# Earlier weight conversions on ScalarE and other PSUM banks for the context, in a graph-network, linear-attention and feed-forward kernel

## The chip, the cores and the metric

The kernel runs on one core of one Trainium2 chip, as a single launch. The metric is the device time of one execution in microseconds (us), lower is better; the time of a version is the median of its runs.

The core has five engines that run side by side and meet only at semaphores: TensorE (PE in the profile; its weight loads are the row PEld), VectorE (DVE), ScalarE (ACT), GpSimd (POOL) and SyncE (SP), which here issues the transfers from memory. TensorE writes to PSUM, which has eight banks.

## The reference, cut to what matters

There are 1250 rows of 512 features. The rows are normalized, and then go through two branches whose results are added to the input; a feed-forward block follows. The change touches the second branch, a linear attention with 8 heads of 64:

```
def mix(x, w_qkv, w_out, b_out, ln_scale):            # x is (1, 1250, 512)
    q, k, v = jnp.split(einsum('bnc,cf->bnf', x, w_qkv), 3, axis=-1)   # then 8 heads of 64
    q = softmax(q, axis=-1) / sqrt(64)                 # over the 64 features of a head
    k = softmax(k, axis=1);  v = v / N                 # over the 1250 rows
    context = einsum('bnhd,bnhe->bhde', k, v)          # 64 x 64 per head
    out = einsum('bhde,bnhd->bhen', context, q)        # back to (1, 1250, 512)
    out = einsum('bnf,fc->bnc', out, w_out) + b_out
    return (out - mean) * rsqrt(var + eps) * ln_scale
```

The first branch is a graph network. It needs `segment_sum(x[src], dst)` twice, over 41250 edges, and the kernel does that as a product with a 1250 x 1250 matrix of edge counts, which it builds itself while the other products run.

## The kernel before, in words

Every product is done with operands that are split in two float16 parts, a high one and a low one, so each block of a product is three matmuls (`passes`, L447 to L457). The 1250 rows are 10 tiles of 125, or 5 chunks of 250.

**Weights.** Ten matrices of 512 x 512 pass one after the other through one staging buffer, in the order `lin, up0, k, q, v, out, down0, up1, down1, gate`. For each, SyncE issues the load into `stage` (L395) once the matrix before has been split, ScalarE scales it in place (L746) and writes the high half to one of three slots (L756), and GpSimd writes the low half (L1639), which frees `stage` for the next load. ScalarE and GpSimd do this at fixed places of their own instruction streams, written out by hand. `wait_slot` keeps ScalarE from writing a slot whose former matrix may still be read.

**The edge counts.** The matrix is built in 25 windows of 50 columns. For a window, VectorE makes the start columns and the one-hot operands (L1105 to L1117, five instructions), TensorE reads the 16 start columns into registers and does one matmul that clears the bank (L440) and 16 small ones (L443), and ScalarE copies the sum out (L767). Windows alternate between banks 6 and 7. Four windows lie among the tiles of `up0`, six in the key stage, ten in the value stage, five in the last stage of the attention.

**The stages around the change**, in order:

- *Key stage*: TensorE does 20 blocks of keys with a window after every third, VectorE moves each block out of PSUM and keeps its maximum. Then VectorE takes the maxima together (`kneg`, L1280), and ScalarE takes four exponentials (L864) that TensorE waits for before it transposes the keys.
- *Query and value stage*: the order of tiles is the list `QV`: queries 0 to 6, then value 0, query 7, value 1, query 8, value 2, query 9, values 3 to 9. They use banks 0 to 3 in turn (family `z`). VectorE subtracts the maximum per head from a query tile (L1291, L1292), ScalarE takes its exponential, VectorE sums it (L1296, L1297), and GpSimd multiplies by the reciprocal (L1657, for all ten tiles, behind the split of `out` in its stream). With each of queries 2 to 6 TensorE transposes two key tiles into banks 4 and 5 (family `x`, L518), ScalarE writes their high half (L780) and VectorE the low one (L1127). A value tile goes out by ScalarE (L877) and VectorE (L1127). The window of a value tile lies behind the next value tile on TensorE (L564), and ahead of the tile's low half on VectorE (L1308).
- *Context*: two halves of 60 matmuls each, then two query tiles transposed by `flip_q` (L508), then four projections (`m`, L587 to L590) of the context with `out`, which use banks 0 and 1 in turn. The halves lie in banks 4 and 5, which the transposed query tiles use next.
- *Last stage of the attention*: ten tiles with the projected matrix, five windows; then the graph layers.

Of the kernel before, what the change touches and what calls it, by code (L numbers as in the profile page):

```python
# [30 lines left out]
T = N // P  # L31
# [42 lines left out]
SLOTS = 3  # L74
# [9 lines left out]
Q_FIRST, KN_LAG = 7, 2  # L84
QV = [("q", _t) for _t in range(Q_FIRST)]
for _t in range(T):
# [6 lines left out]
    "z": [("qv", 2 * T, "dve", 0)],  # L93
# [3 lines left out]
    "x": [("xn", T, "dve", 1), ("up0", T, "dve", 1), ("kn", T, "dve", 1), ("ctx", 2, "dve", 1), ("qt", T, "dve", 1),  # L97
# [44 lines left out]
READER = {"lin": ("t", "lin"), "up0": ("x", "up0"), "k": ("t", "k"), "q": ("z", "qv"), "v": ("z", "qv"), "out": ("n", "m"),  # L142
# [3 lines left out]
def gps_block(nc, dram):  # L146

    with ExitStack() as ctx:
# [203 lines left out]
        def wait_slot(eng, i):  # L352

            if i >= SLOTS:
                family, phase = READER[WEIGHTS[i - SLOTS]]
                eng.wait_ge(full[family], before(family, phase) + entry(family, phase)[1])
# [65 lines left out]
        def _(pe):  # L422
# [147 lines left out]
            for b in range(2):  # L570
                wait_bank(pe, "x", "ctx", b, b)
                for q in range(2):
                    part = slice((2 * b + q) * 128, (2 * b + q + 1) * 128)
                    last = passes(bank("x", b)[:, q * 128:(q + 1) * 128], lambda h, t: v_nat[:, h, t, part],
                                  lambda h, t: k_nat[:, h, t, part], T)
                last.then_inc(full["x"], 1)
# [163 lines left out]
        def _(act):  # L740
# [118 lines left out]
            for i in range(WINDOWS["k"]):  # L859
                window("k", i)  # L860

# [4 lines left out]
            split_weight("v")  # L866

            for i, (kind, t) in enumerate(QV):
                if kind == "q":
# [4 lines left out]
                    nc.scalar.activation(q_nat[:, t, :], q_nat[:, t, :], ACT.Exp, scale=S_XW).then_inc(q_exp, 1)  # L874
                else:
# [3 lines left out]
                    if t == 0:  # L879
                        split_weight("out")  # L880
# [3 lines left out]
            for b in range(2):  # L884
                wait_full(act, "x", "ctx", b)
                for hh in range(2):
                    part = slice(hh * DH, hh * DH + DH)
                    last = nc.scalar.activation(ctx16[part, 0, 2 * b:2 * b + 2, part],
                                                bank("x", b)[part, 0:256].rearrange("p (q d) -> p q d", q=2)[:, :, part],
                                                ACT.Copy, scale=1 / (S_X * S_K))  # L890
                last.then_inc(high["x"], 1)
# [190 lines left out]
        def _(dve):  # L1082
# [233 lines left out]
            for b in range(2):  # L1316
                wait_high(dve, "x", "ctx", b)
                for hh in range(2):
                    part = slice(hh * DH, hh * DH + DH)
                    last = low(ctx16[part, 1, 2 * b:2 * b + 2, part],  # L1320
                               bank("x", b)[part, 0:256].rearrange("p (q d) -> p q d", q=2)[:, :, part],
                               ctx16[part, 0, 2 * b:2 * b + 2, part], 1 / (S_X * S_K))
                last.then_inc(free["x", "dve"], 1)
# [455 lines left out]
```

## Time and profile before

| | before |
|---|---|
| median of 3 runs | 530.96 us (530.7 to 535.82) |
| the profiled execution | 531.56 us, of which the profile's span is 529.8 us |
| TensorE busy | 478.6 us, 90% of the span |
| weight loads of TensorE busy | 363.3 us, 69% |
| VectorE, ScalarE, GpSimd busy | 323.4 us (61%), 251.7 us (48%), 166.1 us (31%) |
| chain that ended last | TensorE 73%, VectorE 13%, ScalarE 9%, issue 3% |
| mean granted clock of TensorE | 0.96 of full speed |

In the profile the place of an instruction is its line in the program, so one of a helper stands for all who call it: L454 is every float16 product, L1127 every low half that is made from a scaled source. A name such as `r` or `late` is a memory region whose parts hold different matrices at different times; `ps` is PSUM.

### The profile page before, as it was taken

What the parts mean: (1) busy time and instruction counts of PE and PEld (TensorE: products, weight loads), DVE (VectorE), ACT (ScalarE), POOL (GpSimd) and SP (SyncE); (2) the same over time, 40 slices, a digit from 0 to 9 for tenths busy, and PEclk for the clock granted to TensorE, in tenths of its full rate; (3) what the DMA queues carried; (4) which work ended last, traced back from release to release, by engine and by line L of the source; (5) the groups of instructions that cost most, each with busy time, mean ns of one, the idle gap of its engine ahead of it and who ended that gap; (6) DMA issues with size and microseconds to landing.
All of it is one profiled execution on the core that took longest, in us unless ns stands there. A gap on an engine that the chain in (4) does not pass through costs nothing.

```text
span 529.8 us, 10016 instructions
## 1 busy us (share of the span) xinstructions
PE 478.6 (90%) x3589; PEld 363.3 (69%) x3589; DVE 323.4 (61%) x737; ACT 251.7 (48%) x526; POOL 166.1 (31%) x176
## 2 busy tenths in 40 slices
PE   2989999997997997997999995999999978989893
PEld 1767558875764665664899993668999857866641
DVE  4667698746969855863453536644333376439777
ACT  4778334137451345153235553534336377743344
POOL 1469154003039103033124990002321323303502
PEclk9989999999999989998899997999999957999998
DMA  8602001200102002002100001000000295000015
GB/s 245 188 2 79 1 12 70 81 1 29 51 2 80 2 1 79 2 6 84 74 0 0 2 1 58 1 0 1 0 0 1 83 396 240 1 0 1 1 41 153
DMA packets 5245, 27.42 MB, mean 52 GB/s; under 512 B 1036, under 2 KB 1161, under 8 KB 3544
## 3 DMA queue, kind: packets, MB, share of 16 engines
q1 hardware_dynamic: 5208, 26.92, 14.7%
q8 instruction: 24, 0.39, 0.3%
q14 instruction: 13, 0.11, 0.1%
HBM read 24.36 MB, written 2.56 MB: 51 GB/s over the span
## 4 chain that ended last, share of the span: by engine, by line
PE 73%; DVE 13%; ACT 9%; issue 3%; POOL 1%; DMA 1%; SPq 0%; ACTq 0%; DVEq 0%
PE ps L454 45%; PE ps L612 17%; PE ps L443 5%; PE ps L704 2%; PE ps L508 2%; DVE r L1126 1%; PE ps L440 1%; ACT wslot L756 1%; DVE r L1578 1%; PE ps L518 1%; DVE stat L1148 1%; DVE r L1590 1%; POOL late L1631 1%; DVE r L1568 1%; ACT late L864 1%
## 5 line engine op out<-in xcount | busy, mean ns | idle before, releaser
L454 PE MATMUL ps<-r,wslot 128*128 128x250 f16 x840 | 97.7, 277 | 4.4 <-DVE r L1126 4.3
L454 PEld LDWEIGHTS ps<-r,wslot 128*128 128x128 f16 x840 | 83.1, 100 | 16.9 <-DVE r L1126 5.9
L612 PE MATMUL ps<-late,r 125*128 (+1 forms) x800 | 89.7, 274 | 3.8 <-issue 3.8
L612 PEld LDWEIGHTS ps<-late,r 125*128 125x128 f16 x800 | 78.8, 99 | 15.0 <-issue 4.5
L1639 POOL TENSOR_TENSOR wslot<-stage,wslot 128x512 f16<-128x512 f32 x32 | 39.4, 1261 | 155.7 <-ACT wslot L756 155.7
L454 PE MATMUL ps<-wslot,r 128*125 128x512 f16 x300 | 69.4, 382 | 0.0
L454 PE MATMUL ps<-wslot,late 128*125 128x512 f16 x240 | 56.3, 389 | 6.3 <-DVE late L1418 5.9
L1667 POOL TENSOR_TENSOR late<-ohs,late 128x250 f16<-128x250 f32 x40 | 25.6, 651 | 99.2 <-ACT late L929 99.2
L454 PEld LDWEIGHTS ps<-wslot,r 128*125 128x125 f16 (+1 forms) x300 | 39.4, 137 | 22.2 <-issue 2.3
L454 PE MATMUL ps<-late,wslot 128*128 x480 | 51.5, 270 | 0.0
L454 PEld LDWEIGHTS ps<-wslot,late 128*125 128x125 f16 x240 | 32.8, 140 | 25.2 <-issue 7.5
L767 ACT ACTIVATE late<-ps 125x500 f16<-125x500 f32 x25 | 14.7, 587 | 74.0 <-PE ps L443 74.0
L454 PEld LDWEIGHTS ps<-late,wslot 128*128 128x128 f16 x480 | 46.7, 97 | 4.5
L1399 DVE TENSOR_SCALAR ohs<-ohs,cols 128x250 f32<-128x250 f32 x40 | 16.1, 405 | 48.3 <-ACT ohs L924 48.3
L924 ACT ACTIVATE ohs<-ps,bias_a 128x250 f32<-128x250 f32 x40 | 18.5, 466 | 37.1 <-PE ps L612 29.9
L1127 DVE SCALAR_TENSOR_TENSOR r<-ps,r 125x512 f16<-125x512 f32 (+1 forms) x30 | 20.4, 684 | 22.7 <-ACT r L780 14.9
L780 ACT ACTIVATE r<-ps 125x512 f16<-125x512 f32 x20 | 12.0, 599 | 39.1 <-PE ps L454 39.1
L1107 DVE TENSOR_TENSOR ohs<-iota,sources 125x2048 f16<-125x2048 f16 x25 | 30.4, 1218 | 0.1
L1438 DVE BATCH_NORM_STATS2 stat<-r x32 | 13.3, 421 | 26.4 <-ACT r L973 26.4
L443 PE MATMUL ps<-ohs 125*128 125x80 f16 x400 | 28.4, 205 | 0.9 <-DVE ohs L1117 0.8
L443 PEld LDWEIGHTS ps<-ohs 125*128 125x128 f16 x400 | 21.9, 99 | 10.0 <-issue 6.7
L973 ACT ACTIVATE r<-ps,cols 128x250 f32<-128x250 f32 x40 | 18.3, 465 | 19.4 <-PE ps L454 19.4
(181 smaller groups left out, 745.3 us busy)
## 6 DMA issues: line engine op xcount, KB each, us to landing
late<-in_tv SPq DMA_DIRECT2D x2, 4096.0 KB, 17.5
x<-in_x SPq DMA_DIRECT2D x5, 448.0 KB
out<-r SPq DMA_DIRECT2D x10, 224.0 KB
stage<-in_w_up SPq DMA_DIRECT2D x2, 1024.0 KB, 5.8
stage<-in_w_down SPq DMA_DIRECT2D x2, 1024.0 KB, 4.7
stage<-in_w_lin SPq DMA_DIRECT2D x1, 1024.0 KB, 6.5
stage<-in_w_k SPq DMA_DIRECT2D x1, 1024.0 KB, 4.8
stage<-in_w_q SPq DMA_DIRECT2D x1, 1024.0 KB, 4.9
```

The lines of the kernel that those rows point to most:

```text
L443: mm_ = nc.tensor.matmul(ps[:, 6 + slot, bass.ds(at[c], SPAN)], oh_s[:, slot, c, :], oh_d[:, slot, c, :], start=False, stop=(c == WC - 1))
L454: last = nc.tensor.matmul(out, stat_(hs, b), mov(hm, b), start=start and n == 0, stop=stop and n == 3 * blocks - 1)
L612: last = nc.tensor.matmul(bank("t", m), u_nat[layer][:, p, h, m * 128:(m + 1) * 128], counts(h)[:, chunk], start=(start and h == 0 and p = ...
L767: nc.scalar.activation(adj[:, :, w * WIN:(w + 1) * WIN], ps[0:P, 6 + w % 2, 0:WK].rearrange("p (d h) -> p h d", h=T), ACT.Copy, accum_out= ...
L924: nc.scalar.activation(act_tmp[:, m, :], bank("t", m), ACT.Identity, bias=bias_a[:, KB * layer + m:KB * layer + m + 1], scale=S_H / S_X).t ...
L973: nc.scalar.activation(gnn_t[:, m, j * CH:(j + 1) * CH], bank("t", m), ACT.Identity, bias=col("b2", KB * layer + m), scale=1 / (S_W * S_H) ...
L1107: nc.vector.tensor_tensor(oh_s[:, slot].rearrange("p c (s r) -> p c s r", r=RUN), iota_s.unsqueeze(1).to_broadcast([P, WC, 128 // RUN, RUN ...
L1127: return nc.vector.scalar_tensor_tensor(out, src, scale, hi, ALU.mult, ALU.subtract)
L1399: nc.vector.tensor_scalar(negative[:, q, :], act_tmp[:, q, :], 0.0, col("conv_a", layer), ALU.min, ALU.mult).then_inc(neg_ready, 1)
L1438: ins = nc.vector.bn_stats(bn_stat[:, m, bass.ts(j, 6)], gnn_t[:, m, bass.ts(j, CH)])
L1639: last = nc.gpsimd.tensor_tensor(wslot[:, i % SLOTS, 1, k, :], stage[:, k * D:(k + 1) * D], wslot[:, i % SLOTS, 0, k, :], ALU.subtract)
L1667: nc.gpsimd.tensor_tensor(a_t[:, 1, m, chunk], act_tmp[:, m, :], a_t[:, 0, m, chunk], ALU.subtract).then_inc(tmp_free, 1)
```

## The change

It has three parts.

1. ScalarE splits `v` two windows before the end of the key stage's windows (after window 4 of 0 to 5) and no longer after the exponentials of the keys. It scales `out` after the exponential of query 5 and writes its high half after that of query 6, and no longer after window 0 of the value stage. GpSimd's stream and SyncE's are as before; they follow as their waits are met.
2. The two halves of the context lie in banks 2 and 3 (`z`), and no longer in 4 and 5 (`x`). The four projections each wait for the half that they read, and no longer all for both.
3. `wait_slot` lets `down0` be written to its slot once the last query is computed, and no longer once the last value is; the place of that split in ScalarE's stream is as before.

```
 USES = {
-    "z": [("qv", 2 * T, "dve", 0)],
+    "z": [("qv", 2 * T, "dve", 0), ("ctx", 2, "dve", 1)],
...
-READER = {... "q": ("z", "qv"), ...}
+READER = {... "q": ("z", "qv", QV.index(("q", T - 1)) + 1), ...}
...
             for b in range(2):
-                wait_bank(pe, "x", "ctx", b, b)
+                wait_bank(pe, "z", "ctx", b, 2 + b)
                 for q in range(2):
                     part = slice((2 * b + q) * 128, (2 * b + q + 1) * 128)
-                    last = passes(bank("x", b)[:, q * 128:(q + 1) * 128], ...)
-                last.then_inc(full["x"], 1)
+                    last = passes(bank("z", 2 + b)[:, q * 128:(q + 1) * 128], ...)
+                last.then_inc(full["z"], 1)
...
             wait_weight(pe, "out")
-            wait_done(pe, "x", "ctx", 2)
             for p in range(KB):
+                wait_done(pe, "z", "ctx", p // 2 + 1)
                 wait_bank(pe, "n", "m", p, p % 2)
...
             for i in range(WINDOWS["k"]):
                 window("k", i)
+                if i == WINDOWS["k"] - 2:
+                    split_weight("v")
...
-            split_weight("v")
 
             for i, (kind, t) in enumerate(QV):
                 if kind == "q":
...
                     nc.scalar.activation(q_nat[:, t, :], q_nat[:, t, :], ACT.Exp, scale=S_XW).then_inc(q_exp, 1)
+                    if t == Q_FIRST - 2:
+                        scale_weight("out")
+                    if t == Q_FIRST - 1:
+                        high_weight("out")
                 else:
...
                     window("v", t)
-                    if t == 0:
-                        split_weight("out")
```

The reads of the context by ScalarE and VectorE, and the semaphores that they raise, are changed from `x` to `z` in the same way.

ScalarE's stream at the end of the key stage, before (L767 copies windows out, L864 is the exponentials of the keys, L746 and L756 scale a matrix and write its high half, L874 is the exponential of a query):

```order
L767 ACTIVATE late,adj_sum<-ps 125x10x50 x6
L864 ACTIVATE late,ksum<-late,kneg 128x1250 x4
L746 ACTIVATE stage<-stage 128x2048
L756 ACTIVATE wslot<-stage 128x2048
L874 ACTIVATE r<-r 125x512 x2
```

The same place of the changed kernel (its line 866 is the former L864, its 875 the former L874):

```order
L767 ACTIVATE late,adj_sum<-ps 125x10x50 x5
L746 ACTIVATE stage<-stage 128x2048
L756 ACTIVATE wslot<-stage 128x2048
L767 ACTIVATE late,adj_sum<-ps 125x10x50
L866 ACTIVATE late,ksum<-late,kneg 128x1250 x4
L875 ACTIVATE r<-r 125x512 x2
```

The pair of L746 and L756 has moved from behind the four exponentials to ahead of the sixth window's copy. Further on in ScalarE's stream, from the key tiles of query 6 on, before (L780 is a key tile, L877 a value tile):

```order
L780 ACTIVATE late<-ps 125x512 x2
L874 ACTIVATE r<-r 125x512
L877 ACTIVATE late<-ps 125x512
L767 ACTIVATE late,adj_sum<-ps 125x10x50
L746 ACTIVATE stage<-stage 128x2048
L756 ACTIVATE wslot<-stage 128x2048
L874 ACTIVATE r<-r 125x512
L877 ACTIVATE late<-ps 125x512
```

The same place of the changed kernel, from the exponential of query 5 on (its line 882 is the former L877):

```order
L875 ACTIVATE r<-r 125x512
L746 ACTIVATE stage<-stage 128x2048
L780 ACTIVATE late<-ps 125x512 x2
L875 ACTIVATE r<-r 125x512
L756 ACTIVATE wslot<-stage 128x2048
L882 ACTIVATE late<-ps 125x512
L767 ACTIVATE late,adj_sum<-ps 125x10x50
L875 ACTIVATE r<-r 125x512
L882 ACTIVATE late<-ps 125x512
```

The scaling of `out` now stands ahead of the last two key tiles, its high half ahead of value 0, and nothing stands between the first value window and query 7. TensorE's instructions are the same in number and order; at the context its waits differ (`free` semaphores of the two families of banks):

```order
-L454 MATMUL ps<-late 128x128 [waits x_free_dve]
+L454 MATMUL ps<-late 128x128 [waits z_free_dve]
 L454 MATMUL ps<-late 128x128 x59
 L508 MATMUL ps<-ident,r 128x125 [waits x_free_dve,q_soft]
...
-L454 MATMUL ps<-wslot,ctx 128x512 [waits n_free_dve,z_free_dve,x_free_dve,w_split]
+L454 MATMUL ps<-wslot,ctx 128x512 [waits n_free_dve,z_free_dve,w_split]
 L454 MATMUL ps<-wslot,ctx 128x512 x2
```

The rows of the transposes (L508) read as before, but the context's own reads no longer count among what their `x` semaphore waits for.

## Rows read from the trace of the kernel before

**Rows 1.** The page, part 4: the chain that ended last, by engine.
```profile
PE 73%; DVE 13%; ACT 9%; issue 3%; POOL 1%; DMA 1%; SPq 0%; ACTq 0%; DVEq 0%
```

**Rows 2.** Timeline of TensorE: start, duration, instruction, count, idle before and its releaser.
```profile
123.17 1.04 PE L518 MATMUL ps<-ident,late 128*125 128x128 f32 x8
124.04 2.75 PE L454 MATMUL ps<-wslot,r 128*125 128x512 f16 x12
129.69 1.21 PE L518 MATMUL ps<-ident,late 128*125 128x128 f32 x8 [2.89 <-DVE late L1127]
```

**Rows 3.** Timeline of ScalarE, key stage to query 5.
```profile
114.24 0.59 ACT L767 ACTIVATE late<-ps 125x500 f16<-125x500 f32 x1 [4.65 <-PE ps L443]
...
121.57 1.89 ACT L746 ACTIVATE stage<-stage 128x2048 f32<-128x2048 f32 x1
...
125.31 1.13 ACT L874 ACTIVATE r<-r 125x512 f32<-125x512 f32 x2
...
137.42 1.08 ACT L780 ACTIVATE late<-ps 125x512 f16<-125x512 f32 x2 [1.82 <-PE ps L518]
```

**Rows 4.** Timeline of VectorE, query 2 and the first key tiles.
```profile
126.79 0.64 DVE L1291 TENSOR_REDUCE qmax<-ps 125x8 f32<-125x512 f32 x1
...
128.07 0.68 DVE L1296 TENSOR_REDUCE qsum<-r 125x8 f32<-125x512 f32 x1
...
128.90 1.24 DVE L1127 SCALAR_TENSOR_TENSOR late<-ps,late 125x512 f16<-125x512 f32 x2
```

**Rows 5.** Timeline of SyncE's queue.
```profile
91.89 0.33 SPq L395 DMA_DIRECT2D stage<-in_w_v  x1
```

**Rows 6.** DMA issues: KB each, median us from issue to landing.
```profile
stage<-in_w_v SPq DMA_DIRECT2D x1, 1024.0 KB, 4.7
```

**Rows 7.** Timeline of GpSimd: the split of out, the ten query tiles.
```profile
154.58 4.50 POOL L1639 TENSOR_TENSOR wslot<-stage,wslot 128x512 f16<-128x512 f32 x4 [24.61 <-ACT wslot L756]
159.04 14.70 POOL L1657 TENSOR_TENSOR r<-r,qsum  x10
```

**Rows 8.** Timeline of VectorE, value windows 0, 1 and 2.
```profile
143.77 0.17 DVE L1105 TENSOR_SCALAR base<-heads 125x16 f32 x1
...
146.14 0.69 DVE L1127 SCALAR_TENSOR_TENSOR late<-ps,late 125x512 f16<-125x512 f32 x1
...
155.54 0.69 DVE L1127 SCALAR_TENSOR_TENSOR late<-ps,late 125x512 f16<-125x512 f32 x1 [4.15 <-ACT late L877]
...
158.30 0.81 DVE L1105 TENSOR_SCALAR base<-heads 125x16 f32 x1
...
162.90 0.68 DVE L1127 SCALAR_TENSOR_TENSOR late<-ps,late 125x512 f16<-125x512 f32 x1
```

**Rows 9.** Timeline of ScalarE, after value window 0.
```profile
150.66 1.90 ACT L746 ACTIVATE stage<-stage 128x2048 f32<-128x2048 f32 x1
```

**Rows 10.** Timeline of TensorE, value stage.
```profile
149.88 5.37 PE L454 MATMUL ps<-wslot,r 128*125 128x512 f16 x24
...
162.38 0.37 PE L440 MATMUL ps<-iota,zeros 1*128 1x500 f16 x1 [0.93 <-issue]
163.12 2.12 PE L443 MATMUL ps<-ohs 125*128 125x80 f16 x16 [0.38 <-DVE ohs L1117]
...
175.26 2.01 PE L443 MATMUL ps<-ohs 125*128 125x80 f16 x16
177.19 2.77 PE L454 MATMUL ps<-wslot,r 128*125 128x512 f16 x12
...
180.21 0.75 PE L443 MATMUL ps<-ohs 125*128 125x80 f16 x16
```

**Rows 11.** Timeline of TensorE, second query transpose behind the context.
```profile
204.03 0.62 PE L508 MATMUL ps<-ident,r 125*128 125x125 f32 x4 [0.93 <-DVE ctx L1127]
```

**Rows 12.** Busy time of each engine by stretch, then granted clock (PEclk), DMA share, GB/s.
```profile
182.00:195.00 13.00, 12.20 (x103) 7.69 (x102) 9.86 (x20) 3.74 (x11) 0.00 (x0) 0.94 0.01 1
195.00:203.00 8.00, 8.00 (x124) 7.87 (x121) 0.58 (x2) 5.12 (x8) 3.60 (x4) 0.88 0.01 2
```

More of the change, by code:

```diff
@@ L139 @@
 assert WINDOWS["up0"] == T - UP_LAG and WINDOWS["k"] == (KB * J - 1) // K_EVERY and WINDOWS["v"] == T and WINDOWS["mix"] < T - 3
-READER = {"lin": ("t", "lin"), "up0": ("x", "up0"), "k": ("t", "k"), "q": ("z", "qv"), "v": ("z", "qv"), "out": ("n", "m"),
+READER = {"lin": ("t", "lin"), "up0": ("x", "up0"), "k": ("t", "k"), "q": ("z", "qv", QV.index(("q", T - 1)) + 1), "v": ("z", "qv"), "out": ("n", "m"),
           "down0": ("t", "down0"), "up1": ("x", "up1"), "down1": ("t", "down1"), "gate": ("t", "gate")}
@@ L354, in wait_slot @@
             if i >= SLOTS:
-                family, phase = READER[WEIGHTS[i - SLOTS]]
-                eng.wait_ge(full[family], before(family, phase) + entry(family, phase)[1])
+                family, phase, *uses = READER[WEIGHTS[i - SLOTS]]
+                eng.wait_ge(full[family], before(family, phase) + (uses[0] if uses else entry(family, phase)[1]))
         def weight(name):
@@ L570, in _ @@
             for b in range(2):
-                wait_bank(pe, "x", "ctx", b, b)
+                wait_bank(pe, "z", "ctx", b, 2 + b)
                 for q in range(2):
                     part = slice((2 * b + q) * 128, (2 * b + q + 1) * 128)
-                    last = passes(bank("x", b)[:, q * 128:(q + 1) * 128], lambda h, t: v_nat[:, h, t, part],
+                    last = passes(bank("z", 2 + b)[:, q * 128:(q + 1) * 128], lambda h, t: v_nat[:, h, t, part],
                                   lambda h, t: k_nat[:, h, t, part], T)
-                last.then_inc(full["x"], 1)
+                last.then_inc(full["z"], 1)
             def flip_q(t):
@@ L888, in _ @@
                     last = nc.scalar.activation(ctx16[part, 0, 2 * b:2 * b + 2, part],
-                                                bank("x", b)[part, 0:256].rearrange("p (q d) -> p q d", q=2)[:, :, part],
+                                                bank("z", 2 + b)[part, 0:256].rearrange("p (q d) -> p q d", q=2)[:, :, part],
                                                 ACT.Copy, scale=1 / (S_X * S_K))
-                last.then_inc(high["x"], 1)
+                last.then_inc(high["z"], 1)
             high_tile_t("qt", q_t, 0, S_Q)
@@ L1320, in _ @@
                     last = low(ctx16[part, 1, 2 * b:2 * b + 2, part],
-                               bank("x", b)[part, 0:256].rearrange("p (q d) -> p q d", q=2)[:, :, part],
+                               bank("z", 2 + b)[part, 0:256].rearrange("p (q d) -> p q d", q=2)[:, :, part],
                                ctx16[part, 0, 2 * b:2 * b + 2, part], 1 / (S_X * S_K))
-                last.then_inc(free["x", "dve"], 1)
+                last.then_inc(free["z", "dve"], 1)
             low_tile_t("qt", q_t, 0, S_Q)
```

6 lines of the change are left out of this document (3 added, 3 removed).

## The prediction

> **What bounds the kernel now.** I read the chain of work that ended last first: it is TensorE for 73% of the span, and VectorE, ScalarE and issue for most of the rest [rows 1]. So an edit that moves work on ScalarE pays only where TensorE stands idle because of it. I then read TensorE's timeline from the key stage to the context for its idle times, and at each the timelines of the engine that ended it. Three places answer to the change. At 129.69 TensorE has stood idle for 2.89 us, until VectorE had made the low half of the first key tile [rows 2]. In the value stage windows 2, 3 and 4 are late: at window 2 TensorE waits 0.93 and 0.38 us, and its 16 small matmuls take 2.12 us, where those of window 5, ready long before, take 0.75 us [rows 10]. And at 204.03 it waits 0.93 us for VectorE to be done with the second half of the context [rows 11].
>
> **Part 1, the split of v.** ScalarE needs 1.89 us to scale and, with the high half, ends 3.74 us after it began: 121.57 to 125.31 [rows 3]. These 3.74 us stand between the exponentials of the keys and those of the queries. In their new place the cover is the idle time of 4.65 us ahead of the last key window's copy at 114.24 [rows 3], from 109.6 to 113.4; so they cost nothing there, and would cost at most 3.74 us if TensorE's windows came closer. The data are there: the load was issued at 91.89 and lands 4.7 us later, at about 96.6 [rows 5, 6].
>
> Without them the first two query exponentials begin at 121.6. VectorE can then start query 2 as soon as TensorE has it, at 123.2 plus about 0.2. It needs 1.28 us for the shift (126.79 to 128.07), 0.83 us for a sum (128.07 to 128.90) and 0.62 us for each low half [rows 4]. First key tile free at 123.4 + 1.28 + 0.83 + 0.62 = 126.1. TensorE does query 3 from 124.04 and is ready for the next transposes at about 126.6 [rows 2]. So the 2.89 us wait goes wholly, and with it the 0.2 us by which the transposes of a stalled pass last longer (1.21 against 1.04 us): **3.1 us**. Next late is nothing: VectorE is then 0.5 us ahead. GpSimd's split of v comes with it, from 125.5 to about 113.5, where VectorE's maximum of the keys (at 116) could be held by it for one of its instructions, 1.12 us (4.50 us for four) [rows 7]. That eats the 0.5 us and some 0.3 us more. Ends: 2.8 and 3.2.
>
> **Part 1, the split of out.** Its two halves go to queries 5 and 6. There ScalarE idles 1.82 us before each pair of key tiles [rows 3], and scaling takes 1.90 us [rows 9], the high half as long: each fits within 0.1 us, with the first value tile perhaps 0.4 us later, which VectorE does not feel since it makes value window 0 first. Where it stood, after window 0 (150.66, 1.90 us twice), it held back the high half of value 1, and VectorE waited 4.15 us for that at 155.54 [rows 8, 9]. That wait goes. But TensorE loses only what makes it late, so I laid the two engines out step by step, all 3.1 us (rounded to 3.2) earlier to begin with:
>
> VectorE starts value window 0 at 140.6. A window takes it 2.37 us alone (143.77 to 146.14), and 4.60 us while GpSimd works through (158.30 to 162.90) [rows 8]. GpSimd splits out from 141.3 to 145.8 and then has six query tiles waiting, at 1.47 us each [rows 7]: it is busy until about 157.6. So I take 4.2, 4.4, 3.7, 2.9 and 2.9 us for windows 0 to 4, between these two ends by GpSimd's share of each. Between two windows lie 2.76 us (155.54 to 158.30) [rows 8], after the last query 1.4. The one-hot operands are then ready at 144.8, 151.9, 158.4, 164.1 and 168.4.
>
> TensorE has value 1 done at 145.8. A pair of tiles is 5.3 us, a window 0.9, or 2.3 when its operands come only just ahead (2.12 or 2.01 against 0.75) [rows 10]. Window 0 at 145.8, window 1 at 152.1, window 2 at 158.6 and late (2.3), value 4 until 163.6, window 3 held to 164.5 and late, value 5 until 169.3, window 4 partly late (1.3). Value 6 starts at 170.6, and before it was at 177.19 [rows 10]. That is 6.6 us earlier, 3.1 of which are known: **3.5 us** for the split of out. Ends: all five windows at 4.60 us give value 6 at 175.5 (1.4 us lost again); never late gives 166.4 (7.6 us won). I take the middle one, since the rows say for how long GpSimd is busy.
>
> From here each value tile costs TensorE more than it costs VectorE, and all later splits and loads hang on TensorE's progress: what follows moves as a block.
>
> **Parts 2 and 3.** With the context in banks of its own, the second query transpose needs nothing from VectorE: 0.93 us go [rows 11]. The projections that follow could begin yet earlier, but their copies queue behind the same reads on ScalarE and VectorE, so the shorter wait for half the context adds nothing: **0.9 us**, ends 0 and 1.9. Banks 2 and 3 were last used by values 8 and 9, which the context waits for anyway. The earlier slot for down0 costs and brings nothing: its split stands behind the last window in ScalarE's stream, when all values have been computed.
>
> **The sum.** 3.1 + 3.5 + 0.9 = 7.5 us. The profiled execution took 531.56 us, so it would be 524.1; the median shown is 0.6 lower, which gives 523.5 us.
>
> **A rule against it.** The trace shows GpSimd's work making VectorE's window 2.23 us longer, which is about 1.5 of its instructions of 1.47 us [rows 7, 8]; the loss sits on the short scalar operations and on the last comparison.
>
> The Trainium skill (SBUF — State Buffer, "SBUF: two separate sides") says that the pair of ports which VectorE and GpSimd share is an exclusive lock, held for a whole instruction, also against a VectorE instruction with two inputs in SBUF. By that rule all five instructions of a window could be held, not only some.
>
> **Rivals.**
> - *VectorE becomes the bound of the value stage.* For: the split of out and the query tiles now meet windows 0 to 4, not 1 to 4. Against: GpSimd has a fixed amount to do. If each window takes 4.60 us the stage gives 1.4 us back: 3.1 - 1.4 + 0.9 = 2.6, or 528.4 us. Chance 0.10.
> - *Each of the five instructions is held.* At half a GpSimd instruction (0.73 us) each, a window is 2.37 + 3.7 = 6.0 us while GpSimd is busy (windows 0 and 1) and 3.1 us after; value 6 then starts at about 173.8, 3.4 us earlier. With the context's 0.9 that is 4.3, or 526.7 us. Against it: 4.60 us is what the row has. Chance 0.07. This is the case of the rule named above.
> - *The windows are in time.* If GpSimd's share is smaller than I have it, up to 10.8 + 0.9 = 11.7 us: 519.3 us. Chance 0.07.
> - *Slower, by the clock.* Between 182 and 203 TensorE was granted its lower level, 1.2 instead of 2.4 GHz, for a part of the time, after a stretch in which it was busy 12.20 of 13 us; over the two stretches that cost 0.06 x 13 + 0.12 x 8 = 1.7 us [rows 12]. Three windows stay late in my count, and idle time at them could bring more such falls. From five more the gain is gone, with six it is 2.7 us slower, 533.7 us. Against: the changed stretch has less idle time than the one before. One fall more or less stays in my range. Chance 0.03.
> - *The split of v misses its gap,* and nothing is saved in front: 7.5 - 3.1 = 4.4, or 526.6 us. Against: both the data and the idle time are in the rows. Chance 0.03.
>
> My forecast has 0.70. Its own range is 521 to 526 (the ends of the key part, 1.7 us of clock, 1.5 us in the value stage). With the rivals, 520.4 to 528.2 holds 8 in 10. About 1% is 5.3 us, what a measurement of this kernel can tell from no change: faster 0.78 (the forecast and the in-time case, little of the others), within it 0.18, slower 0.04.
>
> **What would show it.** In the changed profile: no idle time before the transposes of key tiles 2 and 3, and those at about 126.6; ScalarE's conversion of v between its fifth and sixth key window; no wait of VectorE for value 1's high half; VectorE's windows 0 to 2 near 4 us each; windows 2 and 3 still slow on TensorE; value 6 near 170.6; no wait of the transposes for the context. The forecast is wrong if value 6 starts after 173 or before 168, or if TensorE's granted clock differs over more than some 7 us of the span.

## The result and the profile after

The changed kernel took 525.21 us (median of 4 runs, 524.54 to 526.75); the kernel before took 533.29 us beside it (4 runs, 530.7 to 535.82). The ratio is 0.9857 [0.9812, 0.9903]: faster by 1.4%. Measured again in two later series, the unchanged text of the changed kernel gave 524.55 us at 0.9879 [0.9843, 0.9915] and 524.34 us at 0.9847 [0.9809, 0.9884]. The forecast was 523.5 us, in a range of 520.4 to 528.2.

The profiled execution took 525.78 us with a span of 523.2 us, 6.6 us less than the span of before (529.8). The page's head and its chain by engine:

```profile
PE 477.9 (91%) x3589; PEld 363.3 (69%) x3589; DVE 325.3 (62%) x737; ACT 251.5 (48%) x526; POOL 167.6 (32%) x176
...
PE 79%; DVE 10%; ACT 6%; issue 2%; POOL 1%; DMA 1%; SPq 0%; ACTq 0%; DVEq 0%
```

The chain stands on TensorE for 79% of the span, where it was 73% [rows 1]; what has shrunk is VectorE's part (13% to 10%) and ScalarE's (9% to 6%). TensorE's instructions are the same; the place of ScalarE's conversions and the waits were edited.

**Key and query stage.** ScalarE's timeline around the last key window:

```profile
109.46 1.90 ACT L746 ACTIVATE stage<-stage 128x2048 f32<-128x2048 f32 x1
111.40 1.91 ACT L756 ACTIVATE wslot<-stage 128x2048 f16<-128x2048 f32 x1
114.27 0.59 ACT L767 ACTIVATE late<-ps 125x500 f16<-125x500 f32 x1 [0.96 <-PE ps L443]
...
121.60 1.29 ACT L875 ACTIVATE r<-r 125x512 f32<-125x512 f32 x2
```

The conversion of v sits in what was 4.65 us of idle time [rows 3] and leaves 0.96 us of it; the window's copy starts at 114.27 instead of 114.24, and the first exponentials of the queries at 121.60 instead of 125.31. On TensorE the wait of 2.89 us [rows 2] is gone:

```profile
123.20 1.04 PE L518 MATMUL ps<-ident,late 128*125 128x128 f32 x8
...
126.66 1.04 PE L518 MATMUL ps<-ident,late 128*125 128x128 f32 x8
127.54 2.75 PE L454 MATMUL ps<-wslot,r 128*125 128x512 f16 x12
```

**Value stage.** TensorE, in the same view as rows 10. L440 opens a window, L443 are its 16 small matmuls, whose addresses are read from registers; windows 0 to 4 start in these rows:

```profile
145.79 0.38 PE L440 MATMUL ps<-iota,zeros 1*128 1x500 f16 x1
146.10 0.98 PE L443 MATMUL ps<-ohs 125*128 125x80 f16 x16
...
152.62 1.56 PE L443 MATMUL ps<-ohs 125*128 125x80 f16 x16
...
159.71 1.19 PE L443 MATMUL ps<-ohs 125*128 125x80 f16 x16
...
164.79 0.37 PE L440 MATMUL ps<-iota,zeros 1*128 1x500 f16 x1 [1.16 <-issue]
165.09 2.10 PE L443 MATMUL ps<-ohs 125*128 125x80 f16 x16
167.08 4.19 PE L454 MATMUL ps<-wslot,r 128*125 128x512 f16 x12
...
171.51 0.75 PE L443 MATMUL ps<-ohs 125*128 125x80 f16 x16
172.09 1.27 PE L454 MATMUL ps<-wslot,r 128*125 128x512 f16 x5
```

Value 6 starts at 172.09, 5.1 us earlier than before [rows 10] and 1.5 us later than forecast. Only window 3 still waits. Value 5, at 167.08, lasts 4.19 us where a value tile takes 2.78: TensorE was at its lower level (1.2 GHz) for most of it (mean granted clock 0.57 from 166 to 170). The slow matmuls of windows 0 to 2 are not the clock's: it was 1.00 from 144 to 166.

VectorE, window 0, the first row of window 1 and the low half behind it, and two rows of window 4; L1108, L1110, L1115, L1117 and L1120 are the five instructions of a window:

```profile
140.57 0.17 DVE L1108 TENSOR_SCALAR base<-heads 125x16 f32 x1
140.65 1.22 DVE L1110 TENSOR_TENSOR ohs<-iota,sources 125x2048 f16<-125x2048 f16 x1
141.78 1.12 DVE L1115 TENSOR_SCALAR offsets<-base 1x16 int32<-1x16 f32 x1
...
143.16 1.67 DVE L1120 TENSOR_TENSOR ohs<-iota,rel 125x1280 f16<-125x1280 f16 x1
...
147.50 0.49 DVE L1108 TENSOR_SCALAR base<-heads 125x16 f32 x1
...
151.78 0.68 DVE L1130 SCALAR_TENSOR_TENSOR late<-ps,late 125x512 f16<-125x512 f32 x1
...
167.28 1.01 DVE L1115 TENSOR_SCALAR offsets<-base 1x16 int32<-1x16 f32 x1
...
168.55 0.82 DVE L1120 TENSOR_TENSOR ohs<-iota,rel 125x1280 f16<-125x1280 f16 x1
```

From the start of the base to the start of the low half, windows 0 to 4 last 4.18, 4.28, 4.06, 3.27 and 3.77 us (in the last, 0.42 us is idle time behind the five instructions). The wait of 4.15 us for value 1's high half [rows 8] is gone. GpSimd:

```profile
113.38 4.50 POOL L1642 TENSOR_TENSOR wslot<-stage,wslot 128x512 f16<-128x512 f32 x4 [21.58 <-ACT wslot L756]
141.21 5.75 POOL L1642 TENSOR_TENSOR wslot<-stage,wslot 128x512 f16<-128x512 f32 x4 [23.33 <-ACT wslot L756]
146.92 11.06 POOL L1660 TENSOR_TENSOR r<-r,qsum  x8
161.63 1.94 POOL L1660 TENSOR_TENSOR r<-r,qsum  x1 [3.65 <-DVE qsum L1300]
166.32 1.94 POOL L1660 TENSOR_TENSOR r<-r,qsum  x1 [2.75 <-DVE qsum L1300]
```

Its share of the split of out takes 5.75 us and not 4.50. With eight query tiles it is busy until 157.98, near the forecast (157.6). But the last two query tiles are each released by VectorE's reciprocal (L1300), which stands immediately ahead of a window. So windows 3 and 4 meet one GpSimd instruction each. That I had not seen.

**Context.** TensorE behind it:

```profile
197.97 1.03 PE L508 MATMUL ps<-ident,r 125*128 125x125 f32 x8
198.83 1.46 PE L454 MATMUL ps<-wslot,ctx 128*128 128x512 f16 x6
201.40 1.47 PE L454 MATMUL ps<-wslot,ctx 128*128 128x512 f16 x6 [1.11 <-issue]
```

Both transposes run as one group of 8, with no wait between them, where 0.93 us stood [rows 11].

**The account.** I cut the span at the starts of fixed pieces of TensorE's work. Behind each stretch, in brackets, is an estimate of what the lower level cost TensorE in it, the stretch times one minus its granted clock. It is the most that it can have cost: where TensorE would have waited otherwise, the stretch is not longer by it. The third column is the same kernel in its second series.

| Stretch | before | changed | changed again | gain (changed) |
|---|---|---|---|---|
| start to transposes of key tiles 2, 3 | 129.69 | 126.66 | 125.89 | 3.03 |
| to value 0 | 11.43 | 11.27 | 11.26 | 0.16 |
| to value 6 | 36.07 | 34.16 (1.7) | 33.78 | 1.91 |
| to the context | 17.59 (0.5) | 17.55 | 17.60 | 0.04 |
| to the last attention stage | 16.32 (1.1) | 15.92 (1.8) | 15.92 (1.8) | 0.40 |
| to the graph products | 38.49 (0.8) | 38.31 | 38.04 | 0.18 |
| to down0 | 45.34 (2.7) | 44.38 (1.8) | 44.38 (1.8) | 0.96 |
| to the end | 234.87 (14.1) | 234.95 (14.1) | 234.73 (14.1) | -0.08 |

The first mark moves from run to run: with TensorE's work the same ahead of it and its wait gone, it stood at 125.89 to 126.98 in seven profiles. So single microseconds of it prove little, and I read the stretches, not the marks. The gain ahead of it can be had without that shift, from one pair of transposes to the next: 123.17 to 129.69 before is 6.52 us, 123.20 to 126.66 in the changed kernel 3.46. Experiments 2 and 5, which keep the wait, have 6.53 and 6.52; experiments 4 and 8, without it, 3.46 both.

### The profile page after: what moved, and what is told of

Its sections match the earlier page's. It is cut to its first block, busy times and chain, and to the rows that moved or that the text cites. A ratio compares the mean times of both kernels' runs of the same rounds, so it can differ in the third digit from the quotient of the medians.

```text
span 523.2 us, 10016 instructions
## 1 busy us (share of the span) xinstructions
PE 477.9 (91%) x3589; PEld 363.3 (69%) x3589; DVE 325.3 (62%) x737; ACT 251.5 (48%) x526; POOL 167.6 (32%) x176
## 4 chain that ended last, share of the span: by engine, by line
PE 79%; DVE 10%; ACT 6%; issue 2%; POOL 1%; DMA 1%; SPq 0%; ACTq 0%; DVEq 0%
PE ps L454 50%; PE ps L612 17%; PE ps L443 5%; PE ps L704 2%; PE ps L508 2%; PE ps L440 2%; DVE r L1129 1%; PE ps L518 1%; DVE r L1581 1%; DVE stat L1151 1%; DVE r L1593 1%; POOL late L1634 1%; DVE r L1571 1%; DMA x<-in_x 1%; ACT r L784 1%
## 5 line engine op out<-in xcount | busy, mean ns | idle before, releaser
L1642 POOL TENSOR_TENSOR wslot<-stage,wslot 128x512 f16<-128x512 f32 x32 | 40.6, 1299 | 142.4 <-ACT wslot L756 142.4
L454 PE MATMUL ps<-wslot,r 128*125 128x512 f16 x300 | 70.8, 387 | 0.0
L454 PEld LDWEIGHTS ps<-wslot,late 128*125 128x125 f16 x240 | 32.7, 140 | 25.3 <-issue 7.5
L767 ACT ACTIVATE late<-ps 125x500 f16<-125x500 f32 x25 | 14.7, 587 | 72.3 <-PE ps L443 72.3
L780 ACT ACTIVATE r<-ps 125x512 f16<-125x512 f32 x20 | 12.0, 599 | 39.3 <-PE ps L454 39.3
L1110 DVE TENSOR_TENSOR ohs<-iota,sources 125x2048 f16<-125x2048 f16 x25 | 30.5, 1218 | 0.1
L454 PE MATMUL ps<-late,r 128*125 128x512 f16 x120 | 27.4, 380 | 0.0
L443 PE MATMUL ps<-ohs 125*128 125x80 f16 x400 | 27.0, 204 | 0.1
```

The source lines that it names most:

```text
L443: mm_ = nc.tensor.matmul(ps[:, 6 + slot, bass.ds(at[c], SPAN)], oh_s[:, slot, c, :], oh_d[:, slot, c, :], start=False, stop=(c == WC - 1))
L454: last = nc.tensor.matmul(out, stat_(hs, b), mov(hm, b), start=start and n == 0, stop=stop and n == 3 * blocks - 1)
L767: nc.scalar.activation(adj[:, :, w * WIN:(w + 1) * WIN], ps[0:P, 6 + w % 2, 0:WK].rearrange("p (d h) -> p h d", h=T), ACT.Copy, accum_out= ...
L1110: nc.vector.tensor_tensor(oh_s[:, slot].rearrange("p c (s r) -> p c s r", r=RUN), iota_s.unsqueeze(1).to_broadcast([P, WC, 128 // RUN, RUN ...
L1642: last = nc.gpsimd.tensor_tensor(wslot[:, i % SLOTS, 1, k, :], stage[:, k * D:(k + 1) * D], wslot[:, i % SLOTS, 0, k, :], ALU.subtract)
```

## The experiments

My theory after the result: three waits went, worth 3.1, 3.5 and 0.9 us, and the value stage fell short because the windows' cost had been mis-sized. The rivals were that only one part pays, that the clock takes back what the others bring, and that GpSimd is not what makes the windows long. Medians are given with the ratio to the kernel before, measured beside it.

**1. Only the split of v is moved.**

```diff
                 window("k", i)
+                if i == WINDOWS["k"] - 2:
+                    split_weight("v")
...
-            split_weight("v")
```

> Only the split of v is moved; out, the context's banks and the slots are as before. My theory: the idle time ahead of the transposes of key tiles 2 and 3 goes, so these start at 126.7 instead of 129.7, and everything behind is 3.0 to 3.2 us earlier; the wait of 4.15 us for the high half of value 1 stays. About 0.6% faster than before. The rival, that VectorE's windows take it back: the value stage then starts 3.1 us earlier but value 6 less than 2 us earlier.

526.99 us (526.36 to 527.48), 0.9898 [0.9865, 0.9931]. The mark stands at 126.14. In the value stage VectorE still waits for value 1's high half, and TensorE's windows 2 and 3 are late:

```profile
151.82 0.69 DVE L1128 SCALAR_TENSOR_TENSOR late<-ps,late 125x512 f16<-125x512 f32 x1 [4.15 <-ACT late L878]
```
```profile
158.64 0.37 PE L440 MATMUL ps<-iota,zeros 1*128 1x500 f16 x1 [0.91 <-issue]
159.40 2.12 PE L443 MATMUL ps<-ohs 125*128 125x80 f16 x16 [0.39 <-DVE ohs L1118]
161.44 4.46 PE L454 MATMUL ps<-wslot,r 128*125 128x512 f16 x12
...
168.36 4.46 PE L454 MATMUL ps<-wslot,r 128*125 128x512 f16 x12
```

Two value tiles at 4.46 us instead of 2.78 are 3.4 us of lower clock, and yet the stage lasts 36.24 us, as before (36.07): what TensorE lost to the clock, the next windows would have made it wait. Of the 5.4 us by which this profile's span is shorter (524.4), 3.55 lie ahead of the mark and the rest from the context on, where less was lost to the clock (to the last attention stage 15.30 us, none lost, against 16.32 with 1.1 lost). So by the stretches this part is worth its forecast of 3.1 us. The medians are 5.5 us apart, and even the near end of the interval (0.9931) is 3.7 us: what the rest is, no run shows.

**2. Only the split of out is moved.**

```diff
                     nc.scalar.activation(q_nat[:, t, :], q_nat[:, t, :], ACT.Exp, scale=S_XW).then_inc(q_exp, 1)
+                    if t == Q_FIRST - 2:
+                        scale_weight("out")
+                    if t == Q_FIRST - 1:
+                        high_weight("out")
...
-                    if t == 0:
-                        split_weight("out")
```

> Only the split of out is moved. My theory: TensorE is 3 to 3.5 us earlier at value 6 (177.2 before) and unchanged up to value 1; one fall of the granted clock more or less changes that by 1.4 to 1.7 us. The rival, that VectorE bound by GpSimd gives it all back: value 6 at 176 or later.

531.49 us (527.74 to 534.82, 10 runs), 0.9984 [0.9954, 1.0015]: by itself no difference. Its value stage is shorter, 34.45 us against 36.07: 1.6 us, where 3 to 3.5 were expected. Value 6 starts at 178.48, later than before, so by its mark the expectation failed. What took it back in the profiled execution is the piece ahead, where the wait of 2.9 us is still there:

```profile
129.75 2.04 PE L518 MATMUL ps<-ident,late 128*125 128x128 f32 x8 [2.90 <-DVE late L1129]
131.58 4.82 PE L454 MATMUL ps<-wslot,r 128*125 128x512 f16 x12
```

Behind it the transposes take 2.04 us instead of 1.21 and the query 4.82 instead of 2.75: the granted clock from 129 to 137 was 0.58. That stretch is 14.28 us long against 11.43. In the profile of before the same wait has no such fall behind it. But in experiment 5, which has both splits where they were, it has one again: transposes of 2.04 us, a query of 3.24. So the fall does not need the moved split of out; what the two have in common is the idle time of 2.9 us. Four profiles keep that wait and two have the fall behind it; of the ten without the wait none has. Part of what experiment 1 gained beyond its forecast may lie here, which no run shows. The ten runs of this experiment spread over 7 us.

**3. Only the context's banks and the wait per half.**

```diff
-            wait_done(pe, "x", "ctx", 2)
             for p in range(KB):
+                wait_done(pe, "z", "ctx", p // 2 + 1)
```
(and bank z instead of x at every read and write of the context)

> Only the banks of the context and the wait for half of it are changed. My theory: 0.9 to 1.1 us between the start of the context and the first tile of the last stage of the attention, nothing elsewhere. The rival, that the next wait takes it up (the third projection waits for its bank): the first tile of the last stage is less than 0.4 us nearer to the start of the context.

530.66 us (527.74 to 531.81, 10 runs), 0.9976 [0.9953, 0.9998]. The stretch from the context to the last attention stage is 14.30 us, none of it lost to the clock; before it was 16.32 with 1.1 lost, so 15.2 to 15.3 at full clock (experiment 1, which has the old context, shows 15.30 with none lost). 1.0 us for this part, against 0.9 forecast.

Its value stage, which the edit does not touch, is 36.61 us against 36.07, and VectorE has a row there that no other profile has. Window 2 begins at 158.03; GpSimd's first query tile starts at 158.76, in the same moment as L1107 (L1110 in the changed kernel), and L1107 lasts 2.13 us instead of 1.21 to 1.23:

```profile
158.75 2.13 DVE L1107 TENSOR_TENSOR ohs<-iota,sources 125x2048 f16<-125x2048 f16 x1
```

Four of the five instructions of this window are held, and it lasts 5.51 us, where before it lasted 4.60. In the trace of before the same two start at 159.02 (L1107) and 159.04 (the tile), and L1107 took 1.21 us: a few hundredths of a microsecond seem to decide who is held.

The three ratios of the parts are 1.02, 0.16 and 0.24% below one, together 1.4%: that of the whole. With intervals of 0.2 to 0.3% on either side of each, and the shares so unlike those of the stretches, this agreement shows little.

**4. The changed kernel with the wait for the whole context** (and down0's old slot).

```diff
+            wait_done(pe, "z", "ctx", 2)
             for p in range(KB):
-                wait_done(pe, "z", "ctx", p // 2 + 1)
```

> The changed kernel with two of its edits undone: the projections wait for both halves of the context again, and down0's slot waits for the last value again. My theory: both edits do nothing, so the time and all the marks are those of the changed kernel within 0.2 us. The rival: waiting for half the context is what saves the 1 us at the context, and this kernel is 0.5 to 1 us slower there.

525.52 us (525.13 to 527.52), 0.9883 [0.9845, 0.9921], no difference in time from the changed kernel. But TensorE shows one:

```profile
199.88 1.45 PE L454 MATMUL ps<-wslot,ctx 128*128 128x512 f16 x6 [0.46 <-issue]
202.31 1.05 PE L454 MATMUL ps<-wslot,ctx 128*128 128x512 f16 x4 [0.98 <-DVE late L1130]
```

The first projection waits 0.46 us that it did not wait in the changed kernel, and the stretch is 16.41 us against 15.92. "The shorter wait adds nothing" is wrong: it adds 0.5 us. Two edits are undone here at once; that down0's slot is not what does it is shown by experiments 3 and 5, both with the old slot, which differ by the wait alone. Experiment 3 and, with the new slot, experiments 6 and 7 have this stretch at 14.29 to 14.30 us where the granted clock was full, so the slot brings nothing, as forecast.

**5. Only the banks, with the wait for the whole context.** Experiment 3 with one line as in 4.

> The kernel before with the context in banks 2 and 3, but all projections still waiting for both halves. From the start of the context to the first tile of the last stage it is 15.3 us before and 14.3 with both edits, where the granted clock is full. My first theory, that the shorter wait does nothing, gives 14.3 here. The rival, borne out by small_undone, that each edit is worth half: 14.8.

One execution, 535.07 us, of which 3 us are a late start (the mark stands at 132.73). The stretch is 14.78 us, between 15.30 without this part and 14.30 with all of it. So banks and half-wait give 0.5 us each.

**6. GpSimd does five query tiles before its half of the split of out.**

```diff
-            for name in ("k", "q", "v", "out"):
+            for name in ("k", "q", "v"):
                 split_weight(name)
+            soft_tiles(0, 5)
+            split_weight("out")
+            soft_tiles(5, T)
```
(`soft_tiles` is the former loop over the query tiles, from one tile to another)

> The changed kernel, with GpSimd doing the first five query tiles ahead of the split of out, where it is idle in the changed kernel (118 to 141 us), not behind it. My theory, that GpSimd's work beside VectorE's value windows is what holds the value stage: windows 1 and 2 take VectorE near 3 us instead of 4.2 and 4.1, window 3 is no longer late on TensorE, and value 6 starts 2 to 4 us earlier than in the changed kernel (172.1), so 520 to 523 us on the clock of the first comparison. The rival, that VectorE alone is too slow there or that the matmuls of a window are slow whatever VectorE does: value 6 within 1 us of 172.1.

524.63 us (520.87 to 526.33, 5 runs), 0.9874 [0.9837, 0.9911]. VectorE's windows 1 and 2 shorten from 4.28 and 4.06 to 3.55 and 3.27 us, and the value stage to 32.94 us (34.16 and 33.78 in the changed kernel). Window 3 is late all the same: its 16 matmuls take 2.07 us. So the windows got shorter as expected, but the rest was not met: value 6 starts 1.8 us earlier and not 2 to 4, and the median is that of the changed kernel beside it (524.55). About 1 us of stage is less than the time can tell.

**7. Out is split earlier still: scaled at query 2, high half at query 3; GpSimd does two query tiles, its half of the split, the rest.**

```diff
-                    if t == Q_FIRST - 2:
+                    if t == Q_FIRST - 5:
                         scale_weight("out")
-                    if t == Q_FIRST - 1:
+                    if t == Q_FIRST - 4:
                         high_weight("out")
```
(GpSimd as in 6, with 2 in place of 5)

> As soft_first, but out is scaled after query 2 and its high half written after query 3, and GpSimd does query tiles 0 and 1, then the split of out, then the rest: all of it before value window 0, or nearly. My theory: window 0 takes VectorE 2.4 to 3.3 us instead of 4.2, no window from 0 to 4 is late, and value 6 starts at 166.5 to 168, 4 to 5.6 us earlier than in the changed kernel: about 1% faster than it. The rival, that ScalarE or VectorE is slowed in the query stage instead (its slack there is 0.1 us per query): the transposes of key tiles 4 to 9 start later, and value 6 is less than 3 us earlier.

521.53 us (519.99 to 522.77), 0.9813 [0.9769, 0.9856]; again, in the last series, 520.51 us (520.14 to 522.97), 0.9785 [0.9748, 0.9823]. GpSimd, VectorE and TensorE of the first:

```profile
131.25 4.50 POOL L1642 TENSOR_TENSOR wslot<-stage,wslot 128x512 f16<-128x512 f32 x4 [3.91 <-ACT wslot L756]
...
140.14 1.04 POOL L1659 TENSOR_TENSOR r<-r,qsum  x1 [1.39 <-DVE qsum L1300]
146.47 1.94 POOL L1659 TENSOR_TENSOR r<-r,qsum  x1 [5.29 <-DVE qsum L1300]
```
```profile
142.26 0.15 DVE L1115 TENSOR_SCALAR offsets<-base 1x16 int32<-1x16 f32 x1
...
146.29 1.23 DVE L1110 TENSOR_TENSOR ohs<-iota,sources 125x2048 f16<-125x2048 f16 x1
147.43 1.01 DVE L1115 TENSOR_SCALAR offsets<-base 1x16 int32<-1x16 f32 x1
```
```profile
146.53 0.75 PE L443 MATMUL ps<-ohs 125*128 125x80 f16 x16
...
167.06 1.71 PE L443 MATMUL ps<-ohs 125*128 125x80 f16 x16
```

Window 0 meets no GpSimd work and lasts 2.42 us instead of 4.18; the others meet one instruction each and last 3.26, 3.27, 3.27 and 3.77. (The fifth has 0.42 us of idle time behind its five instructions.) TensorE's windows 0 to 2 are in time, and the stage lasts 30.33 us (30.31 in the repeat). Windows 3 and 4, which were expected in time as well, are late (16 matmuls in 1.59 and 1.71 us), so value 6 starts at 168.69 and not by 168. Against the changed kernel the time is 0.6 and 0.7% lower, not 1%.

**8. More GpSimd work: the changed kernel with ten more products (125x512) ahead of the query tiles.**

```diff
+            pool.wait_ge(got_rows, 32)
+            for _ in range(10):
+                then(nc.gpsimd.tensor_tensor(rows[:, 1, :], rows[:, 1, :], ones[0:P, 0:1].to_broadcast([P, D]), ALU.mult))
             with pool.Fori(0, T) as t_:
```

> The changed kernel with ten more instructions of 512 columns on GpSimd between the split of out and the query tiles (they multiply a row by one and change no result), so that it is busy from 141 to about 177 us. My theory: every window from 0 to 5 takes VectorE 4.1 to 4.6 us, 7.2 us from window to window while there are queries, and value 6 starts at 174 to 177, 2 to 5 us later than in the changed kernel. The rival, that held windows are hidden behind TensorE: value 6 at 172 to 173.

529.42 us (527.6 to 531.4, 10 runs), 0.9958 [0.9934, 0.9983]: most of the gain is gone.

```profile
165.93 0.37 PE L440 MATMUL ps<-iota,zeros 1*128 1x500 f16 x1 [1.75 <-issue]
...
168.84 5.13 PE L454 MATMUL ps<-wslot,r 128*125 128x512 f16 x12
```

VectorE's windows 0 to 5 are all 4.2 to 4.6 us now and value 6 starts at 174.79, in the range expected. A part of the longer stage (36.55 us) is the lower clock, which made value 5 last 5.13 us. But the operands of window 4 came at 172.33, 3.0 us later than in the changed kernel (169.37), so TensorE would have had to wait for them without it. This kernel is the case that the prediction's first rival describes; I had put its value 6 at 175.5.

**9. Query tiles paced: out split as in 7, and each of the last four query tiles on GpSimd waits until VectorE is done with the next value tile,** so that it runs beside VectorE's work on PSUM instead of beside a window.

```diff
+            soft_tiles(2, Q_FIRST - 1)
+            for t in range(Q_FIRST - 1, T):
+                wait_done(pool, "z", "qv", QV.index(("v", t - Q_FIRST + 2)) + 1)
+                soft_tiles(t, t + 1)
```

> As out_early, but GpSimd takes each of query tiles 6 to 9 only when VectorE has ended the window that follows the tile's sum, so that no value window has any GpSimd work beside it. My theory: the single held instruction of windows 1 to 4 (0.85 us each in out_early) goes, every value window takes VectorE 2.4 us, none is late on TensorE (16 matmuls in 0.75 us), and value 6 starts 28.4 to 28.8 us after value 0, against 30.3 in out_early and 33.8 in the changed kernel: about 1.7 us faster than out_early. The rival, that windows 3 and 4 are late because VectorE is, with or without GpSimd (two windows follow at one value tile's distance): value 6 stays at 30 us.

520.65 us (519.78 to 522.0, 6 runs), 0.9779 [0.9744, 0.9814]. GpSimd, first and last of the four:

```profile
148.34 1.04 POOL L1659 TENSOR_TENSOR r<-r,qsum 125x512 f32<-125x512 f32 x1 [8.71 <-DVE late L1130]
...
165.36 1.95 POOL L1659 TENSOR_TENSOR r<-r,qsum 125x512 f32<-125x512 f32 x1 [3.59 <-DVE late L1130]
```

A tile takes 1.04 us beside PSUM work and 1.95 us when it meets a window. TensorE's first four windows take 0.75, 0.75, 0.75 and 0.79 us, the fifth 1.80, and the stage 29.62 us. That is 0.7 us less than in 7, where 1.7 were expected: nearer to the rival (30 us) than to the theory (28.4 to 28.8).

The times don't tell the two apart (520.65 and 520.51 in one series), and the trace shows why. From value 3 on one value tile follows another without a query between, and VectorE's next window begins soon or at once behind the low half, so a tile that is released there runs into it. The third of the four (160.73) holds the base of window 4 for 0.3 us, the last (165.36) the offsets of window 5, which take 1.01 us. TensorE's fifth and sixth windows, 4 and 5:

```profile
164.71 1.80 PE L443 MATMUL ps<-ohs 125*128 125x80 f16 x16
...
169.45 1.33 PE L443 MATMUL ps<-ohs 125*128 125x80 f16 x16
```

In 7 window 5 takes 0.75 us. So the next stretch, from value 6 to the context, is 18.26 us and not 17.58, and gives the 0.7 us back: the two stretches together are 47.88 us here and 47.89 in 7. Pacing moved the late window on by one, it did not remove it.

**10 to 12. Repeats.** The changed kernel twice (beside 6 to 8, and beside 5 and 9), and version 7 once more; the numbers stand above. The fall of the clock at value 5 is absent in the first repeat (value 5 takes 2.77 us, value 6 starts at 170.93) and back in the second (4.26 us).

> The changed kernel again, on the same chip as the three before it. All theories: 0.9857 of the kernel before within 0.005. The profile shows whether the fall of the granted clock at value 5 (1.4 us) comes back at the same place; if it does not, value 6 starts near 170.7.

> The changed kernel, on the same chip as the two before it, as their base: 0.986 to 0.988 of the kernel before.

> out_early again, on the same chip as paced and the changed kernel, to size both steps in time: 0.5 to 0.7% faster than the changed kernel.

In the last series the changed kernel took 524.34 us (523.03 to 526.48, 6 runs). Every run of version 7 (at most 522.97) and of version 9 (at most 522.0) was below every one of these. So both beat both kernels: about 0.7% below the changed one and 2.1 to 2.2% below the one before.

## Why the prediction was right, and where not

**Split of v, 3.1 us: right.** The wait went, and the place came as worked out. The first two stretches gave 3.03 + 0.16 = 3.2 us, the transposes started at 126.66 (forecast 126.6) and took 1.04 us. From the transposes before them, which no shift of the start touches, it is 3.06 + 0.16 = 3.2 us too. What I had feared of GpSimd, that its split at 113.38 would hold VectorE's maximum of the keys, did not come: that instruction took 0.17 us. Experiment 1 has this part alone at 126.14.

**Split of out, 3.5 us: right in kind, too large.** The wait went and the stage got shorter, by 1.9 us in the first profile and 2.3 us in the second, which had no clock fall in it. Three of the terms were mis-sized:

- *TensorE's windows 0 to 2.* I had two prices for a window, 0.9 us in time and 2.3 just behind. There is a slope between them. The operands are ready when L1120 ends. In the changed kernel the 16 matmuls of windows 0 to 3 began 1.3, 0.8, 1.1 and 0.4 us after that and took 0.98, 1.56, 1.19 and 2.10 us; those that began 1.9 us after it or more took 0.75. For the late ones start and duration add up to 2.2 to 2.6 us behind the operands, in the value stage of every profile. So windows 0 and 1, which I had as in time, cost 1.2 and 1.8 us from L440 to the next tile, 0.3 and 0.9 more than I had, and window 2, which I had as late, 1.45, 0.85 less. These errors cancelled: value 4 starts at 160.85, where I had it (158.6 + 2.3). None of the shortfall lies here.
- *VectorE's windows 3 and 4*, 3.3 us to their operands and not 2.9, for the query tiles that it releases itself. The operands came at 164.7 and 169.4, forecast 164.1 and 168.4. In the second profile, whose stage is 1.1 us longer than my 32.7, this is most of it: window 3 ends 0.3 us later from value 0 than I had it, and window 4 costs 1.9 us from L440 to the next tile, where I had 1.3.
- *The clock.* Value 5 lost 1.41 us in the first profile, but in exchange window 4 was in time (0.75 us instead of 1.65 in the repeat). The two stages differ by only 0.4 us.

That GpSimd is what makes windows long is shown both ways: take it away (7, 9; they also move ScalarE's conversion further) and the stage is 3.8 to 4.5 us shorter, or 3.5 to 4.2 against the repeat without a clock fall; add to it (8) and it is 2.4 us longer, with 1.6 us more at the lower level in it. By time alone this part can't be told: alone it gives 0.16% with an interval over zero (2).

**Context, 0.9 us: the size right, the reason half wrong.** It is worth 1.0 us at full clock (3), half from the banks and half from the wait for half the context (4, 5), which I had at nothing. I had argued that the projections' copies queue behind the same reads; but the first projection itself starts 0.46 us earlier. In the changed kernel's profile 0.40 us of it arrive, since 1.8 us were lost to the clock there and 1.1 before. Windows of the changed kernel in that stretch (engines' busy time in the columns, then the granted clock):

```profile
190.00:194.00 4.00, 4.00 (x46) 4.00 (x44) 0.00 (x0) 3.97 (x4) 0.00 (x0) 0.57 0.01 4
194.00:198.00 4.00, 4.00 (x75) 4.00 (x73) 0.58 (x2) 0.72 (x3) 3.75 (x4) 1.00 0.00 0
```

**What I had not in the sum:** 0.96 us between the graph products and down0. TensorE comes there after 3.6 us of idle time (3.8 before) and is at the lower level (granted clock 0.50 from 249 to 254 before, 0.70 from 243 to 248 in the changed kernel); the kernel before lost 2.7 us to it and the changed one 1.8 us. Nothing of the change touches this place. The repeats and experiments 4 and 6 to 9 lose 1.8 us as well, experiment 2 loses 2.7, experiments 1, 3 and 5 lose 1.3. TensorE arrives there between 238.4 and 252.3, and the loss does not go in one direction with that; I can't say by what rule it goes.

**The sum** was 7.5 us; 3.2 + 1.9 + 0.4 of it came in its places, 1.2 in others, less 0.1: 6.6 us of span. That the second profile has 8.2 us less (521.6) shows what one execution is worth. So there is luck in how well the time agrees: the forecast ratio is 523.5 / 530.96 = 0.9860 and the measured one 0.9857, while only 5.5 of the 7.5 us came where I had them. Most of the other 1.1 us went my way by the clock, and with one run more the median of the kernel before was 533.29 and not 530.96, from which I had started.

**The rule held against it.** The traces show that the two engines hold each other for whole instructions: VectorE's offsets instruction (L1115) takes 0.15 us alone and 1.01 us when a query tile is there, and that tile takes 1.94 us instead of 1.04, because L1110 had begun first. But L1110, which also has two inputs in SBUF, took 1.21 to 1.23 us in every window of the value stage but one, and a window under continuous GpSimd work lasted 4.1 to 4.6 us, not 6.0. The one is window 2 of experiment 3, with 2.13 us and a window of 5.51 us: there GpSimd started in the same moment. The Trainium skill (SBUF — State Buffer, "SBUF: two separate sides") has the pair taken by whoever starts first, for the whole instruction. By that sentence the trace agrees. My step from it to "each of the five is held" does not follow, since GpSimd waits in its turn; but L1110 can be held like the others when it loses that race. Only L1117, of 0.30 us, was never held.

**What stays open:** why the clock falls in some executions of one kernel and not in others; and whether the extra gain of experiment 1 is more than that.

## What to carry to other kernels

Before a wait is priced, look at what is late behind it: a freed wait was worth 4.15 us on VectorE and 2 us on TensorE. Work of a helper engine that can hold the main one is best done before the main one is short of time: that shortened the stage by 3.8 us, the moved conversion alone by 1.9. A tile that the main engine releases itself starts exactly where it is in the way. Waiting for a place beside the main engine's work on PSUM (9) kept the tiles apart from the windows only where that work was longer than a tile, and brought no time beyond version 7. After such an edit, add up the next stretch too. And judge a part by its stretch of the trace when its worth is below what a clock fall costs.

## What the runs showed of the hardware

- GpSimd's product of 125x512 f32 took 1.04 us alone, 1.94 us when it met a window, 1.38 us each in a row (11.06 for eight); its four subtractions of 128x512 took 4.50 or 5.75 us. VectorE's instructions that read 125x512 from PSUM (0.67 to 0.69 us) were never longer beside GpSimd in the value stage. One with two inputs in SBUF (1.22 us) was held once, to 2.13 us.
- Sixteen matmuls with addresses from registers took 0.75 us when their operands had been ready for 1.9 us or more, and up to 2.29 us when they had just come.
- A fall to 1.2 GHz in the value stage made one tile of 12 matmuls 4.19 to 5.13 us instead of 2.78. Each time it stood right behind a late window, though not behind every one, and it cost less than it shows (0.4 us instead of 1.4 in the changed kernel), because the windows after it were then in time.
